# Cross-attention and channel mix as one program instead of two phases: batch 0 of the mix interleaved with the last attention slots, and ScalarE scaling the shifted tokens

## The reference, cut to what matters

```python
# x, ctx: (16, 512, 512) fp32; 16 heads of 32
q, k, v = layernorm(x) @ Wq.T + bq, ctx @ Wk.T + bk, ctx @ Wv.T + bv
attn = softmax(causal(q @ k.T * 32**-0.5)) @ v            # per head, mask applied
x = x + tanh(g_xattn) * (attn @ Wo.T + bo)
h = layernorm(x); h_prev = shift(h, one token later, zeros first)
xr = mu_r * h + (1 - mu_r) * h_prev
xk = mu_k * h + (1 - mu_k) * h_prev
r = sigmoid(xr @ W_r.T)
x = x + tanh(g_ffn) * (r * (square(relu(xk @ W_k.T)) @ W_v.T))
```

## Time and profile before

| | |
|---|---|
| median of 3 runs | 2025.04 us |
| the profiled execution's own time | 2026.49 us |
| its span, first to last instruction | 2024.8 us |
| PE busy | 1928.9 us (95%), 11648 matmuls |
| VectorE, ScalarE, GpSimd busy | 1374.1 (68%), 969.1 (48%), 1293.4 (64%) us |
| mean granted PE clock over the span | 0.981 |
| slices 27 to 30 of 40 (50.6 us each): PE busy tenths | 9, 4, 5, 9 |
| the same slices: granted clock in tenths | 9, 6, 7, 9 |
| HBM read and written | 92.06 and 33.59 MB |

### The profile page before, as it was taken

How to read it: one execution, slowest core, us unless ns; L and a number is a source line. 1 busy time by engine, 2 the same in 40 slices (tenths; PEclk the granted TensorE clock), 3 DMA queues, 4 the chain that set the end, 5 groups by cost and what they waited for, 6 DMA issues and landing times. The chain is left out here.

```text
span 2024.8 us, 36616 instructions
## 1 busy us (share of the span) xinstructions
PE 1928.9 (95%) x11648; PEld 1500.2 (74%) x11648; DVE 1374.1 (68%) x3534; ACT 969.1 (48%) x1870; POOL 1293.4 (64%) x1829
## 2 busy tenths in 40 slices
PE   4899999999999999999999999994599999999999
PEld 3677777777777777777777777762488888888887
DVE  3767677777777777777777777764466675656663
ACT  4555555555555555555555555544243434334341
POOL 4566666666666666666666666656277787777771
PEclk9999999999999999999999999996799999999999
DMA  5544554455544455544465454551222223231311
GB/s 183 109 113 120 134 144 118 118 122 132 145 119 120 121 129 149 120 120 121 125 152 122 114 126 121 132 154 51 76 71 98 88 78 109 67 117 65 103 63 63
DMA packets 128665, 229.31 MB, mean 113 GB/s; under 512 B 18656, under 2 KB 20704, under 8 KB 127616
## 3 DMA queue, kind: packets, MB, share of 16 engines
q1 hardware_dynamic: 128512, 227.43, 42.3%
HBM read 92.06 MB, written 33.59 MB: 62 GB/s over the span
## 5 line engine op out<-in xcount | busy, mean ns | idle before, releaser
L701 DVE CUSTOM_DVE_ANT_0 score_ps<-score_ps,causal 128x128 f32<-128x128 f32 (+3 forms) x1024 | 487.5, 504 | 291.1 <-PE score_ps L855 290.1
L533 ACT ACTIVATE probs<-prob_ps 128x512 f32<-128x512 f32 (+1 forms) x768 | 394.3, 528 | 405.0 <-PE prob_ps L879 202.3
L855 PE MATMUL score_ps<-k_stack,q_stack 97*128 97x128 f32 (+3 forms) x1024 | 319.8, 354 | 6.5 <-DVE least L701 2.9
L879 PE MATMUL prob_ps<-q_stack,k_stack 100*128 100x512 f32 (+3 forms) x1024 | 285.6, 320 | 12.6 <-DMA q_stack<-max_rows 7.4
L385 POOL TENSOR_SCALAR_AFFINE_SELECT probs<-probs 128x256 f32<-128x256 f32 x256 | 106.2, 415 | 259.9 <-ACT probs L533 259.8
L396 POOL TENSOR_TENSOR prob_sum<-probs 128x384 f32<-128x384 f32 x256 | 262.7, 1026 | 0.0
L855 PEld LDWEIGHTS score_ps<-k_stack,q_stack 97*128 97x128 f32 x1024 | 189.7, 191 | 53.4 <-issue 13.3
L879 PEld LDWEIGHTS prob_ps<-q_stack,k_stack 100*128 100x128 f32 x1024 | 194.0, 193 | 33.6 <-DMA q_stack<-max_rows 8.9
L399 POOL TENSOR_TENSOR prob_sum<-prob_sum,probs 128x256 f32<-128x256 f32 x256 | 188.5, 736 | 36.7
L389 POOL TENSOR_SCALAR_AFFINE_SELECT probs<-probs 128x256 f32<-128x256 f32 x256 | 104.5, 408 | 159.0 <-ACT probs L533 158.8
L896 PE MATMUL value_ps<-probs,v 128*32 128x512 f32 (+3 forms) x2048 | 154.0, 442 | 13.2 <-POOL prob_sum L399 13.1
(11 more groups left out here) (145 smaller groups left out, 4910.5 us busy)
## 6 DMA issues: line engine op xcount, KB each, us to landing
k_stack<-staged_k_high SPq DMA_DIRECT2D x256, 128.0 KB
q_stack<-staged_q_high SPq DMA_DIRECT2D x256, 128.0 KB, 3.1
tiles<-in_x SPq DMA_DIRECT2D x16, 1024.0 KB, 5.6
k_stack<-staged_k_low SPq DMA_DIRECT2D x128, 128.0 KB
q_stack<-staged_q_low SPq DMA_DIRECT2D x128, 128.0 KB, 3.1
x_io<-in_x SPq DMA_DIRECT2D x16, 1024.0 KB, 7.8
x<-x_io SPq DMA_DIRECT2D x64, 256.0 KB, 2.9
wk_low_room<-x SPq DMA_DIRECT2D x16, 1024.0 KB, 5.5
```

Of the source, the lines that this page charges most:

```text
L533: nc.scalar.activation(probs[:, u % RING, lo:hi], prob_ps[(3 * u + c) % 2][:, 0:hi - lo], ACT.Exp, scale=SCALE).then_inc(exp_done, 1)
L701: nc.vector.tensor_tensor_reduce(out=here, in0=here, in1=causal[:, LATE - P * t:S], scale=-1.0, scalar=3e38, op0=ALU.add, op1=ALU.min, acc ...
L855: last = nc.tensor.matmul(here[:, at:at + P * (t + 1)], q_stack[n][0:MASK_ROW + 1, j, P * t:P * t + P], k_stack[n][0:MASK_ROW + 1, j, 0:P ...
L879: last = nc.tensor.matmul(here[:, at:at + width], k_stack[n][0:ROWS, j, P * k:P * k + P], q_stack[n][0:ROWS, j, P * k:S], start=True, stop ...
```

## The change

The two phases become one function with one block. It has these parts:

- The mix of batch 0 is laid into the last attention slots (LAST_WORK): its layernorm takes the place that "the next batch" has in slots 243 to 251 (tiles are loaded with x1[0] at slot 240, transposed in slots 250 and 251), its eight mixed tiles are made in slots 252 to 255, its k product runs in slots 253 to 256 and its r product in slots 256 to 258. SLOTS ends at N + LAG; the last values, batch 15's output projection, the transposes of batch 1 and the v product of batch 0 follow.
- The mixed tile is now mu * x + (1 - mu) * x_prev. ScalarE makes the second term from the shifted xT (`scale_earlier`), VectorE the sum (`mix_tokens`); GpSimd's delta is gone.
- The layernorm of the mix is applied by ScalarE, no longer by GpSimd. Newton steps stay on GpSimd (16 small instructions, before 14).
- relu is written into the buffer `square` and squared there by VectorE from SBUF alone; before, VectorE read k_ps and relu.
- In the loop over batches ScalarE's queue has the scaling and the casts of the next batch's k tiles between the four tanh; the r tiles and the layernorm follow. The Fori loops are written out over 15 batches.
- The weight loads are moved: W_k at slot 244, W_r and the tile of batch 1 at slot 250, W_v after the last slot. The low part of W_r goes to GpSimd (slots 252 and 253).
- The mix takes over buffers and PSUM banks of the attention; this adds waits for their last readers. The gate of the mix and the two mu rows are loaded at the start of the program (three small DMAs, the tanh of the gate ahead of the exp tables, two small instructions on GpSimd).

Cut to its core:

```diff
+        LAST_WORK = {
+            N - 4: ("", "", ""),
+            N - 3: ("", "fk0 0", "fk0 12"),
+            N - 2: ("fk0 3", "fk1 01", "fk1 23"),
+            N - 1: ("fk2 01", "fk2 23", "fk3 01"),
+            N: ("", "fk3 23", "fr0 01"),
+            N + 1: ("fr0 23", "fr1 01", "fr1 23"),
+            N + 2: ("fr2 0", "fr2 12", "fr2 3"),
+        }
-        SLOTS = range(N + 14)
+        SLOTS = range(N + LAG)
...
         # sync, slot
-                if i == N - 6:
-                    load_ffn()
+                if i == N - 12:
+                    load_ffn("k")
+                if i == N - 6:
+                    load_ffn("r")
+                    load_x(B + 1)
+                if i == N + 1:
+                    for m in range(T):
+                        load_mix_residual(0, m)
...
+            load_ffn("v")
+            load_x(B + 2)
...
         # gpsimd
+                if i in (N - 4, N - 3):
+                    low_part_ffn(1, "r", 2 * (i - N + 4))
+                    low_part_ffn(1, "r", 2 * (i - N + 4) + 1)
...
+            invert_deviations(B + 1)
+            add_residual_bias(B - 1, 0)
+            add_residual_bias(B - 1, 1)
+            for g in range(K):
+                low_part_act(0, g)
...
         # scalar
+            def scale_earlier(e):
+                j, n, k = mix_tile(e)
+                act.wait_ge(xt_copied, T * (j + 1))
+                wait(act, mixed_done, e - 1)
+                nc.scalar.activation(earlier[:, e % 2, 1:S], ffn_xT[:, k, 0:S - 1], ACT.Identity, scale=mu_rest[:, col, k:k + 1])
...
+            copy_r(3)
+            log_sums(N // HG - 1)
+            invert_sums(N // HG - 1)
+            high_part_act(0, 0)
+            high_part_act(0, 1)
+            high_part_attn(N // HG - 1)
+            for m in range(T):
+                apply_layernorm(B + 1, m)
+            split_ffn("v")
+            high_part_act(0, 2)
+            high_part_act(0, 3)
+            for m in range(T):
+                copy_x(1, m)
+            act.wait_ge(r_copied, T)
+            nc.scalar.activation(r_tanh[:], r_tanh[:], ACT.Tanh, scale=0.5).then_inc(r_ready, T)
+            mix_k(1)
+            mix_r(1)
+            for m in range(T):
+                apply_layernorm(B + 2, m)
+            for j in range(1, B):
+                e = 2 * K * (j + 1)
+                relu_k(j, 0)
+                relu_k(j, 1)
+                copy_x(j + 1, 0)
+                copy_x(j + 1, 1)
...
+                gate_r(j, 0)
+                scale_earlier(e)
+                scale_earlier(e + 1)
+                high_part_mix(e)
+                scale_earlier(e + 2)
+                gate_r(j, 1)
+                high_part_mix(e + 1)
+                scale_earlier(e + 3)
+                high_part_mix(e + 2)
+                gate_r(j, 2)
+                high_part_mix(e + 3)
+                gate_r(j, 3)
+                mix_r(j + 1)
+                for m in range(T):
+                    apply_layernorm(B + j + 2, m)
...
         # vector
+            def mix_tokens(e):
+                dve.wait_ge(scaled, e + 1)
+                nc.vector.scalar_tensor_tensor(out=mixed[:, e % 2, :], in0=ffn_xT[:, k, :], scalar=mu[:, col, k:k + 1],
+                                               in1=earlier[:, e % 2, :], op0=ALU.mult, op1=ALU.add).then_inc(mixed_done, 1)
+            add_output(B - 1, 0)
+            add_output(B - 1, 1)
+            low_part_ffn(2, "v")
+            add_output(B - 1, 2)
+            add_output(B - 1, 3)
+            mix_k(1, False)
+            combine(0, 0)
+            combine(0, 1)
+            take_stats(B + 2)
+            mix_r_and_combine(0, 2)
+            for j in range(1, B):
+                for g in range(K):
+                    square_k(j, g)
+                if j + 1 < B:
+                    mix_k(j + 1, j + 2 < B)
+                    mix_r_and_combine(j, 0)
...
         # tensor
+            for k in range(K):
+                project_fr(0, 3, k)
+            values(N // HG - 1)
+            for m in range(2):
+                for k in range(K - 1):
+                    project_o(B - 1, m, k)
+            for m in range(2):
+                project_o(B - 1, m, K - 1)
+            for m in range(2, T):
+                for k in range(K):
+                    project_o(B - 1, m, k)
+                transpose_x(B + 1, 2 * m - 4)
+                transpose_x(B + 1, 2 * m - 3)
+            for m in range(T):
+                for k in range(K):
+                    project_fv(0, m, k)
+            for j in range(1, B):
+                for g in range(K):
+                    for k in range(K):
+                        project_fk(j, g, k)
+                    if j + 1 < B and g in (1, 2):
+                        transpose_x(B + j + 1, 2 * g - 2)
+                        transpose_x(B + j + 1, 2 * g - 1)
...
```

More of the change, by code:

```diff
@@ L18, with shared_room @@
 RSQRT_SEED = float(0x5F3759DF)
-LN_STEPS = 14
-NORM_STEPS = LN_STEPS + 2
+NORM_STEPS = 16
 def wait(engine, semaphore, count):
-    if not isinstance(count, int) or count > 0:
+    if count > 0:
         engine.wait_ge(semaphore, count)
[L29 to L42, removed]
+def shared_room(nc, ctx, shape, *names):
+    tensors = []
+    for name in names[:-1]:
+        with nc.sbuf_tensor(name, shape, F32R) as tensor:
+            tensors.append(tensor)
+    return *tensors, ctx.enter_context(nc.sbuf_tensor(names[-1], shape, F32))
 def exact_product(nc, out, stationary, moving, steps, first=True, last=True):
@@ L57, in exact_product, with gated_layer @@
     return done
[L60 to L84, removed]
+def gated_layer(nc, x, ctxT, mask, g_xattn, wqT, bq, wkT, bk, wvT, bv, woT, bo, g_ffn, ffn_wT, mu_k, mu_r, x1, mask_bias, out):
     B, S, D = x.shape
@@ L152, in attention_phase @@
         newton = sb("newton", [P, 4, T])
+        mu = sb("mu", [P, 2, K])
+        mu_rest = sb("mu_rest", [P, 2, K])
+        ffn_gate = sb("ffn_gate", [P, 2])
+        x_in, ffn_xT = x_room[1], x_room[0]
+        earlier, mixed = tiles[:, 0:2, :], tiles[:, 2:4, :]
         score_ps = [psum(f"score_ps{n}") for n in range(2)]
@@ L956, in project_o @@
                     pe.wait_ge(w_low, 4)
-                last = exact_product(nc, bank(f"o{m}")[:], lambda k: [part[:, k, P * m:P * m + P] for part in attn],
+                last = exact_product(nc, o_bank(b, m)[:], lambda k: [part[:, k, P * m:P * m + P] for part in attn],
                                      lambda k: [part[:, k, :] for part in w["o"]], [k], k == 0, k == K - 1)
@@ new lines, in project_fr @@
+            def project_fr(j, m, k):
+                if m == 0:
+                    pe.wait_ge(mix_low, 2 * K * j + K + k + 1)
+                    pe.wait_ge(ffn_low["r"], k + 1)
+                if k == 0 and j == 0 and m < 2:
+                    pe.wait_ge(scores_read, T * N)
+                elif k == 0 and j == 0:
+                    pe.wait_ge(r_copied, m - 1)
+                elif k == 0:
+                    pe.wait_ge(r_ready, T * j + m - 1)
+                last = exact_product(nc, r_ps[m % 2][:], lambda k: [part[:, k, P * m:P * m + P] for part in mix["r"]],
+                                     lambda k: [part[:, k, :] for part in ffn_w["r"]], [k], k == 0, k == K - 1)
+                if k == K - 1:
+                    last.then_inc(fr_done, 1)
```

774 lines of the change are left out of this document (399 added, 375 removed).

## The result

The kernel after takes 1966.81 us (median of four runs, 1966.01 to 1967.85) against 2025.01, a ratio of 0.9716 [0.9701, 0.973]: 58 us gained where 45 were forecast, just below the low end of the range.

What follows compares the result with a forecast made beforehand. PE was taken to bound the mix without a hole, leaving gains only in the dip: batch 1's k product at 1447.1 against 1492.15, 45 us, gives 1981.5 from the execution's 2026.49 or 1980.0 from the median; forecast 1981, range 1969 to 1996.

Steps and rivals of the forecast that it cites:

- Loop: Batches of the mix from batch 1's k product on: unchanged at 35.35 us each, the added ScalarE work costing nothing.
- Start: Program start: an added load issue on SP delays the kernel by 0 to 1.5 us, 0.5 taken.
- DMA queue: Row maxima's copy near slot 253: moving two 1 MB loads removes the 5.6 us stall, at worst 2 us left.
- Slots 252 to 255: Last attention slots: VectorE sets the pace, 24.7 us of work plus 3.6 of contention, 28.3 us together.
- rival 2: Contention decides the seam: 18 instructions pay 0.43, cast waits 3, batch 1 delay 5; gain 34, 1991 us; chance 0.12.
- r and the last values: Slots 256 to 258: 18 k steps 12.6, values 3.4, last probabilities 2.1, together 18.1 us; GpSimd's 13.15 wait goes.
- Tail of batch 15: Last values' end at 1411.8 to v of batch 0 near 1426.0: output projection, two k steps, two tiles, 16 transposes.
- The y's chain: v of batch 0, before tile 2: PE waits 6.6 us for the first y, then loses 1.7 to a slower clock.
- Batch 1, 1.5 us late: k tile 2 of batch 1 waits for a relu queued behind batch 2's layernorm: 1.5 us, between 0 and 5.
- The loop's y in time: Each loop batch: y of v tile 0 comes at about 28.6 us, PE wants it at 29.8; 1.1 to spare.
- rivals 3 and 5: Late y per loop batch: 3, PE waits 1 us, 1995 us, chance 0.07; 5, over 3.2 us, slower, chance 0.03.
- Rival 1: Seam tighter: no contention, clock loss or batch 1 delay, half the tanh stall; gain 55 us, 1971 us; chance 0.13.

Runs made afterwards that it cites:

- e10: Kernel before with an unused piece of 1504 bytes per partition behind the channel mix's first tensor: 2012.45 us, ratio 0.994.
- e11: Kernel before with an unused piece of 480 bytes per partition behind the channel mix's first tensor: 2011.79 us, ratio 0.9934.
- e13: Kernel before with an unused piece of 224 bytes per partition behind the channel mix's first tensor: 2009.16 us, ratio 0.9919.
- e14: Kernel before with two of the four 1 MB loads (W_v and x1[0]) issued at slot 253 instead of 250: 2019.36 us, ratio 0.9972.
- e1: Kernel before with an unused piece of 32 bytes per partition behind the channel mix's first tensor: 2022.14 us, ratio 0.9989.
- e17: Kernel before with the unused 224 bytes in the mix and 32 more unused bytes ahead of every tensor: 2010.77 us.

## Why the prediction was wrong, and where it was right

- **Loop, "behind that point I expect the same 35.35 us per batch".** This step failed and made the miss: 34.46 us measured, 13.3 us over 15 batches. The reasoning, that what is done on other engines can't shorten a batch in which PE has no hole, was right. I took the spacing of 0.234 us as a constant of the matmul, and it was a property of the buffers' places, which the change moved. Unused bytes alone in before (e10, e11, e13) show that this is the step: no instruction changed, and 34.46 us a batch. No row of before alone showed it; the rows of the attention, at 0.23 too, seemed to confirm the constant.
- **Start, "between 0 and 1.5 us; I take 0.5".** Sign wrong. ScalarE did start later, but the attention came out 3.5 us earlier, and why is open. I priced the issues and didn't ask whom the delayed instructions would now miss or meet.
- **DMA queue.** Right: no stall at the place of the 5.63 us, and e14 shows its cause.
- **Slots 252 to 255, 28.3 us.** Mis-sized: 31.2, within the 26 to 32 named. I summed VectorE's work as if it never waited. Its work was less than the sum, 25.5 us, and its waits, which I put at nothing, were 5.7; the 3.3 of them for ScalarE's casts between a mixed tile and its low part rival 2 had, at 3.
- **r and the last values, 18.1 us.** Right to the tenth.
- **Tail of batch 15, 14.2 us.** 16.4 in the profiled execution and 15.2 to 15.3 in the nine others. I took 5.1 us from the end of the values to the last low part of the attention output, as in before; PE went on after 6.2 (1408.47 to 1414.66), since that low part now takes 1.76 us instead of 0.75. It takes 1.72 to 1.77 in all ten, and GpSimd is making its own low parts beside it:

```profile
1411.54 2.53 POOL L497 TENSOR_TENSOR kact<-square,kact 128x512 fp32r<-128x512 f32 x2
...
1412.85 1.76 DVE L992 SCALAR_TENSOR_TENSOR attn_low<-inverse,columns,attn_high 128x512 fp32r<-128x512 f32 x1 [0.79 <-ACT attn_high L634]
```

This contention the sum put at nothing, and it is the 1.0 us that all ten have. The other 1.2 is the clock of one execution: behind a wait of 1.8 us, which all ten have, PE ran at half spacing until 1418.1 here, with a mean granted clock of 0.90 over this tail, and at full spacing with 1.00 in the nine others. "As before" was also misread: in before PE has three k steps in that place (1412.32 to 1414.68), not six, and so stood 2.83 us.

- **The y's chain, 6.6 us and 1.7 for the clock.** Measured 5.59 and a stretch of half spacing until 1441.9; the two together came out as forecast. The tanh over 2048 columns took 1.92 us (1.9 taken). The table load is followed by the tanh 1.29 us behind its start, without a further drain: here the trace and the page's 1.38 us on top (the Trainium skill, ScalarE: Activation LUTs, What ACT_TABLE_LOAD costs) differ, and the trace decides.

ScalarE, kernel after:

```profile
1425.83 1.28 ACT L881 ACT_TABLE_LOAD   x1
1427.12 1.92 ACT L881 ACTIVATE r_tanh<-r_tanh 128x2048 f32<-128x2048 f32 x1
```

- **Batch 1, 1.5 us late.** 2.3, with PE standing 0.41 us for batch 2's layernorm and 1.17 for the relu.
- **The loop's y in time (rivals 3 and 5).** Neither happened. VectorE and PE, kernel after, in batch 2:

```profile
1509.10 0.68 DVE L1034 SCALAR_TENSOR_TENSOR probs<-r_tanh,value_ps 128x512 f32<-128x512 f32 x1
```
```profile
1510.34 0.39 PE L41 MATMUL value_ps<-ffn_wv_high,kact 128*128 128x512 f32 x1
```

The y ends at 1509.78, 0.56 us before v tile 2 begins; I had 1.1 to spare.

The range had room for a tighter seam, none for a faster loop, since I took a PE without holes as a floor. Of what would show it right all came but the 35.35 us. Rival 1 (1971) has the time nearest to the measured one, but by none of its conditions: the contention, the clock's loss, batch 1's delay and the tanh stall were all there. That nearness is luck.

## What to carry to other kernels

An engine that is busy without a hole still has a rate; read it from start-to-start times, or from the count of matmuls in a fixed window, and treat it as something that a change of buffers can move. When a kernel's buffers are laid out anew, compare that rate between stages that do the same product. A transfer that everyone waits for should not be issued behind large ones that nobody needs yet: here that alone was 5.4 us. And a wait removed in front of an engine is a gain only if the next release, here the statistics of batch 2, is not fixed by something else.

## What the runs showed that I had not expected

- In the channel mix three fp32r matmuls (128 rows, 512 columns) take 0.680 us when their two SBUF operands begin a multiple of 256 bytes apart, and 0.697 to 0.700 us at 32, 64 or 128 bytes off (the k product 0.684, and 0.691 in e1): 0.89 of 35.35 us, 2.5% of a batch in which PE is the bound. The attention's projections don't follow it.
- Moving every tensor by 32 bytes together (e17) changed neither that nor the total (2010.77 against 2009.16 us).
- Executions of the same attention differ by up to 5 us in where a late head group begins, so one profile against one profile can mislead by that much.
- The same wait of 1.8 us in the tail of batch 15 is followed by half spacing in one of ten executions and by full spacing in nine.
